# Bias rows in four row groups, the zero key's term inside pv, fewer waits, spare products, and a new order of all engines

## The chip, the cores and the metric

The kernel runs on one core of one Trainium2 chip. The core has five engines that run side by side and meet only through semaphores: TensorE (PE in the profile, with its weight loads as PEld), VectorE (DVE), ScalarE (ACT), GpSimd (POOL) and SyncE (SP), which here issues all the transfers. The metric is the device time of one execution in microseconds; less is better.

## The reference

One layer of an audio tower on x of shape 8 x 256 x 128 in float32. Cut to what matters:

```python
zf, zi, zh = x @ Wf + bf, x @ Wi + bi, x @ Wh + bh
diff = softplus(-zf) - softplus(-zi)
log_f, log_i = -softplus(diff), -softplus(-diff)
log_val = concatenate([log(0.5), log_i + log_g(zh)]); a_star = concatenate([0, log_f])
h = exp(a_star + cumlogsumexp(log_val - a_star))        # 257 rows: row 0 is new

n = layernorm(h)                                        # attention, 8 heads of 16
q, k, v = n @ q_w.T, ...kv of the other half of the batch...
h = h + softmax(q k / sqrt(128)) v                      # 257 keys, key 0 among them

n = layernorm(h)                                        # 16 experts, top 2, and a shared one
z = swiglu(n @ shared_w1 + b1) @ shared_w2 + b2
cw = two largest of softmax(n @ gate_w + gate_b), made to sum to 1
y = sum over experts of cw * (swiglu(n @ expert_w1 + b1) @ expert_w2 + b2)
h = h + y + z
```

As row 0 of h is the same 0.5 everywhere, its normalised row is zero: key 0 has score 0 and value 0, and adds only exp(-max) to each denominator. That is the zero key. The output's row 0 needs a small computation of its own for 8 columns (the pieces whose names begin with z and that carry no unit).

## The kernel before

Features lie on the 128 partitions, tokens along the free axis. The batch is cut into 4 units of two sequences (512 columns). A unit goes through three phases: the recurrence (`z`, `lsum`, `e3`, `lp`, `t`, `d`, `hg`, `l`, `al`, `w`, `mscan`, `dw`, `ed`, `sscan`, `lf`, `ef`, `h1`), the attention (`center`, `var`, `rs`, `xn`, `q`, `k`, `v`; then for each sequence s and half c of the keys or queries `mx` with row maxima `mr`, `mz`, the transpose `nmt`, `nm`, `e0`, scores `st`, exponentials `pt`, `o0`, `pv`, `den`, `on`, `h2`), and the experts (`center`, `var`, `gate`, `r1`, `rexp`, `r2`, `cwb`, then 13 chunks of gate and up halves `g` and `u` with their copies `ge`, `ue`, clips, `th`, `gg`, `vc`, `te`, seven `down` steps, `yo`, `out`, `store`). Unit 0 comes first, and later units are laid over it.

Each of these is a piece. The order in which an engine runs its pieces is written out in the table `AT`, one place per piece and engine, as a planner left it; `order()` sorts the pieces by it. `BANK_OF` gives each PSUM bank use its bank, in the order of PE. There are 8 banks; `ps.take` waits until the last user has released one. So no engine chooses anything at run time: each runs its list, and where its next piece waits, everything behind it waits as well.

A float32 product is issued as two passes on PE, each a weight load and a MATMUL; a gate or up half is three float32r products (high and low parts). Score products (`mx`, `st`) use 32 of the 128 rows of the array, four of them side by side in four row groups; `pv` products use 32 columns each, four side by side in four column groups. Other products use the whole array.

The weights `w1` arrive raw. For each of seven parts of up to 512 columns, `wp` adds on PE the bias row (a 2-row product with `bsel`) to the raw part (an identity product), and ACT and DVE split the sum into `w1h` and `w1l`. `o0` writes the zero key's part of the denominators, with all 128 columns of the array, into the bank in which `pv` then accumulates; it is a piece of its own with its own place in the order.

SP's queue issues, in this order: x of unit 0, the first constants, the other constants, x of unit 1, `w1a`, `w1b`, x of unit 2, `w2`, x of unit 3. Lines in the trace: L1146 is every ordinary product (`mm`), L1149 every transpose (`turn`), so tiles tell the pieces apart: `bank<-pt,cst` with 128*128 is the identity product of `wp`, `bank<-tr,cst` with 2*128 its bias product, `bank<-h,cst` the first `center`, `bank<-kt,qt` is `mx` and `bank<-qt,kt` is `st` (the stationary operand comes second), `bank<-e,cst` is `o0`, `bank<-pt,vpad` and `bank<-pt,cst` with 128*32 are `pv`, `xh` and `xl` with `w1h` and `w1l` the gate and up halves, `tr,w` the `down` steps, `zxs` is `zg` and `zy,w` is `zd`.

Of the kernel before, what the change touches and what calls it, by code (L numbers as in the profile page):

```python
# [51 lines left out]


# [5 lines left out]
def unit_pieces(u):  # L59
# [4 lines left out]
    for s in range(2):  # L64
# [14 lines left out]
    f += [("yo", u), ("out", u), ("store", u)]  # L79
    z = []  # L80
# [7 lines left out]
SETUP_PIECES = [(n, 0, k) for k in range(W1_PARTS) for n in ("wp", "w1h", "w1l")] + [("w2s", 0)]  # L88
# [14 lines left out]
def takes_part(engine, piece):  # L103
# [12 lines left out]
    if name in PART_BY:  # L116
# [21 lines left out]
    ),  # L138
# [58 lines left out]
def filled_by(piece):  # L197
# [1253 lines left out]
```

## Time and profile before

| | us |
|---|---|
| median of 3 runs | 304.44 |
| lowest and highest run | 303.33, 305.41 |
| the profiled execution, its own time | 303.86 |
| its span in the profile | 302.0 |
| PE busy | 275.3 |
| DVE busy | 239.7 |
| ACT busy | 188.6 |
| POOL busy | 118.4 |
| mean granted clock of PE, 1 is 2.4 GHz | 0.945 |

The profile is of one execution. Times in it count from the start of the span. The profiled execution took 1.86 us more than its span. A busy time says that an engine had work, not that the work was at full speed: the granted clock stands beside it.

### The profile page before, as it was taken

What the parts mean: (1) busy time and instruction counts of PE and PEld (TensorE: products, weight loads), DVE (VectorE), ACT (ScalarE), POOL (GpSimd) and SP (SyncE); (2) the same over time, 40 slices, a digit from 0 to 9 for tenths busy, and PEclk for the clock granted to TensorE, in tenths of its full rate; (3) what the DMA queues carried; (4) which work ended last, traced back from release to release, by engine and by line L of the source; (5) the groups of instructions that cost most, each with busy time, mean ns of one, the idle gap of its engine ahead of it and who ended that gap; (6) DMA issues with size and microseconds to landing.
All of it is one profiled execution on the core that took longest, in us unless ns stands there. A gap on an engine that the chain in (4) does not pass through costs nothing.

```text
span 302.0 us, 5217 instructions
## 1 busy us (share of the span) xinstructions
PE 275.3 (91%) x1766; PEld 167.0 (55%) x1766; DVE 239.7 (79%) x421; ACT 188.6 (62%) x298; POOL 118.4 (39%) x84
## 2 busy tenths in 40 slices
PE   2994996689989999989999999999979999999993
PEld 1421343446546775554676685447748659767641
DVE  1096645997499989889999699999887977689991
ACT  2849698969768766643688954636877485325051
POOL 2002546480041586063009176200943920391920
PEclk9995798579999999999999999999999996899998
DMA  6800000000000000000010000000000100000011
GB/s 226 358 0 0 0 1 1 2 0 2 2 0 4 0 2 0 0 3 0 2 36 3 0 2 2 0 0 3 0 2 1 37 0 2 1 0 0 2 35 35
DMA packets 3373, 5.78 MB, mean 19 GB/s; under 512 B 266, under 2 KB 2450, under 8 KB 3218
## 3 DMA queue, kind: packets, MB, share of 16 engines
q1 hardware_dynamic: 3348, 5.46, 5.0%
q8 instruction: 15, 0.25, 0.3%
q14 instruction: 10, 0.08, 0.1%
HBM read 4.40 MB, written 1.05 MB: 18 GB/s over the span
## 4 chain that ended last, share of the span: by engine, by line
PE 75%; DVE 11%; issue 7%; ACT 5%; DMA 1%; POOL 0%; DVEq 0%; SPq 0%; ACTq 0%; POOLq 0%
PE bank L1146 73%; DVE mxt L901 3%; PE bank L1149 2%; DVE tr L998 1%; DMA cst<-in_consts 1%; DVE yr L966 1%; ACT qt L635 1%; DVE tr L1018 1%; DVE qt L912 1%; DVE vr L976 1%; ACT pt L672 1%; DVE yo L1028 0%; ACT z L575 0%; ACT al L601 0%; DVE mxt L907 0%
## 5 line engine op out<-in xcount | busy, mean ns | idle before, releaser
L523 POOL TENSOR_TENSOR vr<-vr,cwb 128x1024 f32<-128x1024 f32 x24 | 63.3, 2652 | 16.5 <-DVE vr L976 14.0
L1146 PE MATMUL bank<-tr,w 128*128 128x512 f32 (+1 forms) x104 | 47.8, 599 | 0.0
L901 DVE TENSOR_REDUCE mxt<-bank 128x2 f32<-128x512 f32 x64 | 40.4, 685 | 9.3 <-PE bank L1146 9.0
L724 ACT ACTIVATE tr<-yr,fpar 128x1024 f32<-128x1024 f32 (+1 forms) x28 | 30.1, 1088 | 26.1 <-PE bank L1146 14.1
L1146 PE MATMUL bank<-xh,w1h 128*128 128x512 f32 x104 | 46.3, 446 | 0.0
L966 DVE TENSOR_SCALAR yr<-bank,fpar 128x512 f32<-128x512 f32 x52 | 39.4, 801 | 5.8 <-PE bank L1146 5.7
L1146 PE MATMUL bank<-xh,w1l 128*128 128x512 f32 x104 | 41.5, 400 | 0.0
L1146 PE MATMUL bank<-xl,w1h 128*128 128x512 f32 x104 | 41.5, 399 | 0.0
L998 DVE SCALAR_TENSOR_TENSOR tr<-tr,yr 128x1024 f32<-128x1024 f32 (+1 forms) x28 | 36.6, 1324 | 5.3 <-ACT tr L724 5.3
L672 ACT ACTIVATE pt<-bank 128x512 f32<-128x512 f32 x64 | 33.8, 602 | 9.1 <-PE bank L1146 9.1
L517 POOL TENSOR_SCALAR vr<-vr,fpar 128x1024 f32<-128x1024 f32 x12 | 15.2, 1267 | 48.6 <-ACT vr L711 48.6
L1018 DVE TENSOR_TENSOR tr<-tr,vr 128x1024 f32<-128x1024 f32 x24 | 31.8, 1338 | 0.3
L1146 PEld LDWEIGHTS bank<-tr,w 128*128 128x128 f32 (+1 forms) x104 | 19.1, 190 | 21.4 <-issue 20.0
L1146 PE MATMUL bank<-kt,qt 32*128 32x256 f32 x256 | 21.2, 449 | 7.7 <-DVE mxt L901 6.0
L1146 PEld LDWEIGHTS bank<-xh,w1h 128*128 128x128 f32 x104 | 20.0, 192 | 7.9 <-issue 4.4
L976 DVE TENSOR_SCALAR vr<-bank,fpar 128x512 f32<-128x512 f32 x28 | 21.6, 804 | 3.2 <-PE bank L1146 3.1
L1146 PE MATMUL bank<-pt,cst 128*32 128x256 f32 (+2 forms) x270 | 23.8, 390 | 0.0
L560 ACT ACT_TABLE_LOAD x18 | 23.1, 1283 | 1.0 <-PEq L1444 0.7
L1146 PEld LDWEIGHTS bank<-kt,qt 32*128 32x128 f32 x256 | 13.6, 209 | 17.7 <-issue 10.9
L1146 PEld LDWEIGHTS bank<-xl,w1h 128*128 128x128 f32 x104 | 20.0, 193 | 4.6 <-issue 1.2
L1146 PEld LDWEIGHTS bank<-xh,w1l 128*128 128x128 f32 x104 | 19.9, 191 | 4.7
L1146 PE MATMUL bank<-qt,kt 32*128 32x256 f32 x256 | 19.1, 414 | 3.4 <-DVE yr L966 1.9
(182 smaller groups left out, 431.9 us busy)
## 6 DMA issues: line engine op xcount, KB each, us to landing
pt<-in_w1a SPq DMA_DIRECT2D x1, 1672.0 KB, 9.2
xt<-in_x SPq DMA_DIRECT2D x4, 256.0 KB, 7.4
out<-osb SPq DMA_DIRECT2D x8, 128.0 KB, 1.9
w<-in_w SPq DMA_DIRECT2D x1, 832.0 KB, 10.7
cst<-in_consts SPq DMA_DIRECT2D x1, 552.5 KB, 5.1
cst<-in_consts SPq DMA_DIRECT2D x1, 193.5 KB, 4.2
tr<-in_w1b SPq DMA_DIRECT2D x1, 26.1 KB
out<-zo SPq DMA_DIRECT2D x1, 4.0 KB
```

Of the source, the lines that this page charges most:

```text
L517: g.tensor_scalar(v_, v_, fpar[:, UHI, r:r + 1], fpar[:, ULO, r:r + 1], ALU.min, ALU.max).then_inc(S["ucg"], 1)
L523: g.tensor_tensor(vr[:, n % NV, :, :], vr[:, n % NV, :, :], cwb[:, u % 2, :].unsqueeze(1).to_broadcast([P, 2, W]), ALU.mult).then_inc(S["v ...
L560: nc.scalar.add_instruction(mybir.InstLoadActFuncSet(name=nc.get_next_instruction_name(), act_func_set_id=number, ins=[], outs=[]))
L672: last = a(pt[:, n % NPT, 2 * t:2 * t + 2, :].rearrange("p i t -> p (i t)"), ps.bank("st", u, s, c, t)[:, :], ACT.Exp, scale=SCORE_SCALE)
L724: a(halves(k, tr, n % NT), halves(k, yr, n % NY), ACT.Tanh, scale=fpar[:, HA, r:r + 1]).then_inc(S["th"], 1)
L901: last = v.tensor_reduce(top_of, ps.bank("mx", u, s, c, t)[:, :].rearrange("p (i t) -> p i t", i=2), AX_X, ALU.max)
L966: last = v.tensor_scalar(yr[:, n % NY, c % 2, :], ps.bank("g", u, c)[:, :], fpar[:, GHI, r:r + 1], fpar[:, GLO, r:r + 1], ALU.min, ALU.max)
L976: last = v.tensor_scalar(vr[:, n % NV, c % 2, :], ps.bank("u", u, c)[:, :], fpar[:, UHI, r:r + 1], fpar[:, ULO, r:r + 1], ALU.min, ALU.max)
L998: v.scalar_tensor_tensor(t, t, 1.0, halves(k, yr, n % NY), ALU.add, ALU.mult).then_inc(S["gg"], 1)
L1018: v.tensor_tensor(t, t, halves(k, vr, n % NV), ALU.mult).then_inc(S["tev"], 1)
L1146: return nc.tensor.matmul(out_, lhsT, rhs, start=start, stop=stop, **k)
L1149: return nc.tensor.matmul(out_, data, ident, start=True, stop=True, is_transpose=True)
```

## The change

Five things.

1. `wp` becomes two pieces in place of seven: the identity products of four (then three) parts, then their bias products, part k in row group k mod 4. The bias rows `w1b` are laid out on partitions 0, 32, 64 and 96 and come by four transfers. `bsel` has its two rows in each row group.
2. `o0` is no longer a piece: `pv` with c = 0 takes the bank and writes the zero key's part by four products of 32 columns each.
3. A gate or up half waits for `xl` only if it is the first of its unit on PE, and for parts of `w1` only in unit 0.
4. Eight spare pieces in unit 0, each two products over 256 columns with the weights and x that lie there, into a bank that PE itself releases. Nothing reads the result. Each waits for one event, by `SPARE`.
5. The tables `AT` and `BANK_OF` are new throughout.

```diff
+SPARE = (("m", 2), ("s", 2), ("sq1", 1), ("rs1", 1), ("mz", 1), ("mz", 2), ("nm", 2), ("lden", 1))
...
-            a += [("o0", u, s)] * (c == 0) + [("pv", u, s, c)]
+            a += [("pv", u, s, c)]
...
+    if u == 0:
+        a += [("spare", 0, i) for i in range(len(SPARE))]
...
-SETUP_PIECES = [(n, 0, k) for k in range(W1_PARTS) for n in ("wp", "w1h", "w1l")] + [("w2s", 0)]
+SETUP_PIECES = [("wp", 0, 0), ("wp", 0, 1)] + [(n, 0, k) for k in range(W1_PARTS) for n in ("w1h", "w1l")] + [("w2s", 0)]
...
+FIRST_HALF = [next(p for p in order("P") if p[0] in "gu" and p[1] == u) for u in range(UNITS)]
...
-            sp.dma_start(w1_row, w1b_in).then_inc(s_w1b, 16)
+            for t in range(PAIRS):
+                sp.dma_start(w1_row[32 * t:32 * t + 2, :], w1b_in[2 * t:2 * t + 2, :]).then_inc(s_w1b, 16)
...
-            def wp(u, k):
+            def wp(u, g):
                 pe.wait_ge(s_const, 16)
                 pe.wait_ge(s_w1a, 16)
-                pe.wait_ge(s_w1b, 16)
-                ps.take(pe, "wp", 0, k)
...
-                mm(o, ident, w1_raw[:, cols], stop=False)
-                ps.fill(mm(o, const("bsel")[0:2, :], w1_row[:, cols], start=False), "wp", 0, k)
+                pe.wait_ge(s_w1b, 16 * PAIRS)
+                parts = range(PAIRS * g, min(PAIRS * g + PAIRS, W1_PARTS))
+                cols = [slice(k * W, min((k + 1) * W, W1COLS + E)) for k in range(W1_PARTS)]
+                for k in parts:
+                    ps.take(pe, "wp", 0, k)
+                    mm(ps.bank("wp", 0, k)[:, 0:cols[k].stop - cols[k].start], ident, w1_raw[:, cols[k]], stop=False)
+                for k in parts:
+                    n = cols[k].stop - cols[k].start
+                    rows = slice(32 * (k % PAIRS), 32 * (k % PAIRS) + 2)
+                    ps.fill(mm(ps.bank("wp", 0, k)[:, 0:n], const("bsel")[rows, :], w1_row[rows, g * W:g * W + n], start=False), "wp", 0, k)
+
+            def spare(u, i):
+                ge(pe, *SPARE[i])
+                ps.take(pe, "spare", 0, i)
+                o = ps.bank("spare", 0, i)
+                ps.fill(mm(o[:, 0:T], wtok[:, 0:P], xt[:, 0, 0:T]), "spare", 0, i)
+                ps.release(mm(o[:, T:W], wtok[:, 0:P], xt[:, 0, T:W]), "spare", 0, i)
...
-            def o0(u, s):
-                ps.released(pe, "nmt", u, s)
-                ps.take(pe, "o0", u, s)
-                ps.fill(mm(ps.bank("o0", u, s)[:, T:W], const("e0sel"), e0[:, s, :], start=True, stop=False, skip_group_check=True),
-                        "o0", u, s)
...
+                if c == 0:
+                    ps.released(pe, "nmt", u, s)
+                    ps.take(pe, "o0", u, s)
+                    for t in range(PAIRS):
+                        last = mm(o[32 * t:32 * t + 32, T:W], const("e0sel")[:, 32 * t:32 * t + 32], e0[:, s, :], start=True, stop=False,
+                                  skip_group_check=True)
+                    ps.fill(last, "o0", u, s)
...
-                ge(pe, "xl", u + 1)
-                for k in sorted({(2 * c + kind) * P // W, ((2 * c + kind + 1) * P - 1) // W}):
-                    ps.released(pe, "wp", 0, k)
+                if not AT or (name, u, c) == FIRST_HALF[u]:
+                    ge(pe, "xl", u + 1)
+                if u == 0:
+                    for k in sorted({(2 * c + kind) * P // W, ((2 * c + kind + 1) * P - 1) // W}):
+                        ps.released(pe, "wp", 0, k)
```

The tables, read out as orders, for the stretches of which the text speaks (a name, then the unit, then sequence and half or chunk):

```
PE before, from the start: z0.1 z0.0 z0.2 z1.0 lsum1 z1.2 lsum0 z1.1 wp0.2 wp0.1 wp0.0 wp0.3 center0.1 z2.1 z2.0
  var0.1 lsum3 z2.2 wp0.4 k0 wp0.6 z3.0 z3.1 wp0.5 lsum2 v0 q0 z3.2 mx0.0.0 mx0.0.1 mx0.1.0 mx0.1.1 nmt0.0
  center1.1 st0.0.0 var1.1 o00.0 nmt0.1 st0.0.1 pv0.0.0 st0.1.0 pv0.0.1 st0.1.1 k1 v1 q1 o00.1 pv0.1.0 mx1.0.0
  pv0.1.1 mx1.0.1 mx1.1.0 center0.2 center2.1 nmt1.0 var0.2 mx1.1.1 var2.1 o01.0 st1.0.0 gate0 nmt1.1 v2 g0.5
PE after: z0.0 z0.1 z0.2 z1.1 z1.2 lsum0 z1.0 lsum1 wp0.0 center0.1 spare0.1 spare0.0 spare0.2 var0.1 wp0.1 k0
  q0 spare0.3 v0 mx0.0.0 z2.0 z2.1 z2.2 lsum2 mx0.0.1 mx0.1.0 nmt0.0 spare0.4 st0.0.0 z3.1 st0.0.1 lsum3 z3.2
  mx0.1.1 z3.0 pv0.0.0 pv0.0.1 nmt0.1 spare0.6 spare0.5 center1.1 st0.1.0 spare0.7 var1.1 st0.1.1 pv0.1.0 k1 q1
  pv0.1.1 mx1.0.0 v1 mx1.0.1 center0.2 mx1.1.0 var0.2 nmt1.0 st1.0.0 mx1.1.1 gate0 st1.0.1 pv1.0.0 u0.0 u0.1 g0.0
  cwb0 g0.1
DVE after, from the start: t0 d0 l0 hg0 w0 mscan0 dw0 lf0 sscan0 h10 w2s0 w1l0.0 ... xn0.1 xsum0 w1l0.4 l1 w1l0.5
  w1l0.6 w1 mscan1 dw1 (mr0.0.0) sscan1 (mr0.0.1) mr0.1.0.0 mz0.0 mr0.1.0.1 nm0.0 mr0.1.0.2 mr0.1.0.3 l2
  mr0.1.1.0 w2 mr0.1.1.1 mscan2 dw2 mr0.1.1.2 mr0.1.1.3 mz0.1 sscan2 nm0.1
PE before, the end: ... down3.3 down3.4 down3.5 down3.6 out3, with zg after var3.2 and zd0 after u3.8
PE after, the end: down3.2 down3.3 zcw0 zg0.0 ... zg0.12 down3.4 down3.5 down3.6 out3 zd0 zout0
DVE after, the end: gg3.6 te3.6 zclip0 yo3 zgg0 zte0 zy0
```

In the order before, DVE runs `w2s0` ahead of `h10`, and ACT runs `ed0` ahead of `ef0`; after, both pairs are exchanged.

## Rows read from the trace of the kernel before

**Rows 1.** the page, part 1: busy us, share of the span, instructions

```profile
PE 275.3 (91%) x1766; PEld 167.0 (55%) x1766; DVE 239.7 (79%) x421; ACT 188.6 (62%) x298; POOL 118.4 (39%) x84
```

**Rows 2.** the page, part 4: the chain that ended last, by engine

```profile
PE 75%; DVE 11%; issue 7%; ACT 5%; DMA 1%; POOL 0%; DVEq 0%; SPq 0%; ACTq 0%; POOLq 0%
```

**Rows 3.** stages: us, busy us of PE, PEld, DVE, ACT, POOL; PE clock, DMA, GB/s

```profile
23.00:34.00 11.00, 6.78 (x9) 2.90 (x10) 7.29 (x12) 8.48 (x14) 5.52 (x4) 0.53 0.00 0
34.00:50.00 16.00, 14.31 (x52) 6.09 (x50) 7.18 (x13) 14.95 (x25) 7.75 (x6) 1.00 0.00 1
50.00:64.00 14.00, 10.28 (x68) 6.05 (x68) 13.34 (x24) 9.81 (x15) 8.32 (x6) 0.51 0.01 1
64.00:100.00 36.00, 33.29 (x344) 20.04 (x341) 28.63 (x65) 28.97 (x57) 8.73 (x9) 1.00 0.01 2
...
250.00:262.00 12.00, 12.00 (x58) 10.66 (x58) 7.71 (x36) 4.46 (x8) 1.70 (x2) 0.72 0.01 2
```

**Rows 4.** timeline of PE, 19 to 43 us: start, us, instruction, count, wait before

```profile
19.51 1.12 PE L1146 MATMUL bank<-tr,cst 2*128 2x512 f32 x2
...
21.62 1.12 PE L1146 MATMUL bank<-tr,cst 2*128 2x512 f32 x2
27.22 2.04 PE L1146 MATMUL bank<-h,cst 128*128 128x512 f32 x2 [4.48 <-issue]
...
41.42 1.02 PE L1146 MATMUL bank<-pt,cst 128*128 128x512 f32 x2
42.38 1.12 PE L1146 MATMUL bank<-tr,cst 2*128 2x512 f32 x2
```

**Rows 5.** timeline of DVE, 25 to 27 us

```profile
25.33 0.99 DVE L1035 TENSOR_SCALAR w<-w,fpar 128x1536 f32<-128x1536 f32 x1
...
26.44 0.68 DVE L864 TENSOR_TENSOR h<-state,rl 128x512 f32<-128x512 f32 x1
```

**Rows 6.** timeline of PE, the first score products

```profile
48.56 1.15 PE L1146 MATMUL bank<-kt,qt 32*128 32x256 f32 x16 [1.40 <-ACT vpad L655]
51.13 2.09 PE L1146 MATMUL bank<-kt,qt 32*128 32x256 f32 x16 [1.42 <-DVE mxt L901]
```

**Rows 7.** timeline of PE, 76 to 80 us

```profile
76.33 0.59 PE L1146 MATMUL bank<-e,cst 128*128 128x256 f32 x2
76.86 1.07 PE L1146 MATMUL bank<-pt,vpad 128*32 128x256 f32 x16
...
78.72 1.15 PE L1146 MATMUL bank<-kt,qt 32*128 32x256 f32 x16
79.80 1.07 PE L1146 MATMUL bank<-pt,vpad 128*32 128x256 f32 x16
```

**Rows 8.** the page, part 5: the row maxima on DVE

```profile
L901 DVE TENSOR_REDUCE mxt<-bank 128x2 f32<-128x512 f32 x64 | 40.4, 685 | 9.3 <-PE bank L1146 9.0
```

**Rows 9.** timeline of PE, where experts' products start, and two in between

```profile
94.84 0.48 PE L1146 MATMUL bank<-xh,w1h 128*128 128x512 f32 x1
...
127.42 0.39 PE L1146 MATMUL bank<-xl,w1h 128*128 128x512 f32 x1
127.65 0.39 PE L1146 MATMUL bank<-xh,w1l 128*128 128x512 f32 x1
...
149.93 0.50 PE L1146 MATMUL bank<-xh,w1h 128*128 128x512 f32 x1
```

**Rows 10.** timelines of PE and DVE, short z steps and the end

```profile
274.45 2.96 PE L1146 MATMUL bank<-zy,w 128*128 128x8 f32 x26
...
290.42 6.17 PE L1146 MATMUL bank<-tr,w 128*128 128x512 f32 x14
297.44 0.66 PE L1149 MATMUL bank<-cst,yo 128*128 128x128 f32 x4 [0.85 <-DVE yo L1028]
...
257.16 0.26 DVE L1094 SCALAR_TENSOR_TENSOR zy<-zy 128x104 f32<-128x104 f32 x1
...
296.63 0.75 DVE L1028 SCALAR_TENSOR_TENSOR yo<-bank,cst,h2n 128x512 f32<-128x512 f32 x1 [1.81 <-PE bank L1146]
```

More of the change, by code:

```diff
@@ L124 @@
     "P": (
[13 rows of a table removed]
[12 rows of a table added]
     ),
     "A": (
[10 rows of a table removed]
[10 rows of a table added]
     ),
     "V": (
[13 rows of a table removed]
[13 rows of a table added]
     ),
     "G": (
[3 rows of a table removed]
[3 rows of a table added]
     ),
     "S": (
-        0, 1, 3, 4, 2,
+        0, 1, 2, 3, 4,
     ),
@@ L203, in filled_by @@
         return [("y0", u)]
+    if name == "pv":
+        return [("o0", u, numbers[0])] if numbers[1] == 0 else []
+    if name == "wp":
+        return [("wp", 0, k) for k in range(PAIRS * numbers[0], min(PAIRS * numbers[0] + PAIRS, W1_PARTS))]
     if name == "zg":
         return [("zg", 0)] if numbers[0] == 0 else []
-    one_bank = ("wp", "z", "lsum", "center", "var", "q", "k", "v", "nmt", "o0", "gate", "cwb", "g", "u", "out",
+    one_bank = ("spare", "z", "lsum", "center", "var", "q", "k", "v", "nmt", "gate", "cwb", "g", "u", "out",
                 "zv", "zc", "zvar", "zgate", "zcw", "zd", "zout")
@@ L318, in build @@
         w1_raw = pt[:, :, :, :].rearrange("p a b c -> p (a b c)")[:, 0:W1COLS + E]
-        w1_row = tr[0:2, :, :, :].rearrange("p a b c -> p (a b c)")[:, 0:W1COLS + E]
+        w1_row = tr[:, :, :, :].rearrange("p a b c -> p (a b c)")[:, 0:2 * W]
         memory = [ctx.enter_context(nc.psum_tensor(f"bank{i}", [P, 512], F32)) for i in range(BANKS)]
@@ L1151, in _ @@
             wtok = const("wtok")
-            def wp(u, k):
+            def wp(u, g):
                 pe.wait_ge(s_const, 16)
                 pe.wait_ge(s_w1a, 16)
-                pe.wait_ge(s_w1b, 16)
-                ps.take(pe, "wp", 0, k)
-                cols = slice(k * W, min((k + 1) * W, W1COLS + E))
-                o = ps.bank("wp", 0, k)[:, 0:cols.stop - cols.start]
-                mm(o, ident, w1_raw[:, cols], stop=False)
-                ps.fill(mm(o, const("bsel")[0:2, :], w1_row[:, cols], start=False), "wp", 0, k)
+                pe.wait_ge(s_w1b, 16 * PAIRS)
[14 more added lines that the diff above has]
+                ps.release(mm(o[:, T:W], wtok[:, 0:P], xt[:, 0, T:W]), "spare", 0, i)
             def z_(u, j):
@@ L1370, in _ @@
             run("P", {"z": z_, "lsum": lsum, "center": center, "var": var, "q": q_, "k": k_, "v": v_, "mx": mx, "nmt": nmt,
-                      "st": st, "o0": o0, "pv": pv, "gate": gate, "cwb": cwb_, "g": gate_half, "u": up_half, "down": down,
-                      "out": out_, "zv": zv, "zc": zc, "zvar": zvar, "zgate": zgate, "zcw": zcw, "zg": zg, "zd": zd, "zout": zout, "wp": wp})
+                      "st": st, "pv": pv, "gate": gate, "cwb": cwb_, "g": gate_half, "u": up_half, "down": down,
+                      "out": out_, "zv": zv, "zc": zc, "zvar": zvar, "zgate": zgate, "zcw": zcw, "zg": zg, "zd": zd, "zout": zout, "wp": wp, "spare": spare})
 def layout(inputs):
@@ L1406, in layout @@
     shift = np.stack([np.zeros_like(shift), shift], axis=1).reshape(-1)
-    w1b = np.stack([w1[0], np.concatenate([shift, np.zeros(E, np.float32)])])
+    w1b = np.zeros((PAIRS, 2, 2 * W), np.float32)
+    for k in range(W1_PARTS):
+        cols = slice(k * W, min((k + 1) * W, W1COLS + E))
+        at = slice(k // PAIRS * W, k // PAIRS * W + cols.stop - cols.start)
+        w1b[k % PAIRS, :, at] = np.stack([w1[0], np.concatenate([shift, np.zeros(E, np.float32)])])[:, cols]
     w2e, w2s = f("L0_ffn_expert_w2")[:, :, perm], f("L0_ffn_shared_w2")[:, perm]
@@ L1423, in layout @@
     bsel = np.zeros((P, P), np.float32)
-    bsel[0, 1:] = -1.0
-    bsel[1, 0] = 1.0
+    bsel[0::32, 1:] = -1.0
+    bsel[1::32, 0] = 1.0
     parts = {
@@ L1435, in layout @@
     consts = np.concatenate([parts[n] for n in CONSTS], axis=1)
-    arrays = {"x": x, "consts": consts, "w1a": w1a, "w1b": w1b, "w2": w2.reshape(P, -1)}
+    arrays = {"x": x, "consts": consts, "w1a": w1a, "w1b": w1b.reshape(2 * PAIRS, -1), "w2": w2.reshape(P, -1)}
     return {k: np.ascontiguousarray(a) for k, a in arrays.items()}
```

99 rows, old and new, of tables (AT, BANK_OF, BY) are left out of this document.

## The prediction, made before the change was run

> **What bounds the kernel now.** I began with the page: TensorE (PE) is busy 275.3 of 302.0 us, VectorE (DVE) 239.7, ScalarE (ACT) 188.6 [rows 1], and the chain that ended last lies on PE for 75% and on DVE for 11% [rows 2]. A busy PE need not be a fast one, so the stages came next, with the granted clock beside them [rows 3]. Outside four stretches PE is full at the upper level, 2.4 GHz. The four are: from 23 to 34 us PE works 6.78 us, nearly all at half clock (1.2 GHz); from 34 to 50 it idles 1.7 us; from 50 to 64 it works 10.28 us at half clock and idles 3.7; from 64 to 100 it idles 2.7. Late, from 250 to 262, the granted clock is 0.72, so 6.7 us were at half. Half clock costs half of the busy time: 3.4 + 5.1 us in front, about 3.3 late. Idle in front is 8.1 us. So 16.6 us are to be had before 100 us, and anything elsewhere must come off PE's own work.
>
> Then the order of time. PE runs out of work at 22.74, idles 4.5 us, and resumes at 27.22 with the product that reads h1 of unit 0 [rows 4]. The other hole is the unit's row maxima: the first two batches of score products start at 48.56 and 51.13, behind waits of 1.40 and 1.42 us [rows 6], and two more like them follow by 57.6, the later ones waiting for the DVE reductions that free banks. DVE takes 0.69 us for each of 64 such reductions [rows 8], about 0.62 from start to start, so a batch of four costs it 2.5 us while PE needs 1.08 [rows 7]. PE is starved there, not full, and slow besides.
>
> **The change part by part.**
>
> *Bias rows in four row groups.* A product of 512 columns is two passes of 0.43 us (fourteen of them take 6.17 [rows 10]), 0.86 in all. An identity product that a bias product follows takes 0.96, and from one bias product over an identity product to the next it is 2.11 [rows 4], so a change of shape costs 0.19, there and back 0.39, of which the product behind bears 0.1 (left out below on both sides). Four of the seven parts stand ahead of the hole, 8.4 us in all up to 22.74, and three behind it, two of 2.0 and a short one of 1.2: 5.2. After, four identity products and one group of bias products cost 3.4 + 1.05 = 4.5, and the last three 2.2 + 1.05 = 3.2. That the group lasts as long as one product I take from the score products, whose 16 passes over 256 columns in four row groups take 1.08 [rows 7]: four at a time. The first saving, 3.9 us, only widens the hole in front of 27.22: it is worth nothing. The second is worth **-2.0**. Bound if the groups do not overlap: 0. The rows now come by four transfers in place of one, and the x of units 2 and 3 and w2 are queued behind three more issues on SP. The first of them is read after 40 us in the new order: hidden by the work in front; the four themselves are waited for ahead of the first identity product, at 14.3 us; should they land later, the hole behind covers 3.9 us and more.
>
> *The way to h1 of unit 0.* The scaling of w2 (1.27 us of DVE, from 25.33) stands ahead of the h1 product at 26.44 [rows 5]; now it stands behind. But ACT's exponentials are exchanged (ef before ed), which puts the second scan some 0.6 us later. I take the hole to end at 27.0; bounds 26.1 and 27.6. -0.2.
>
> *Spare pairs.* Each is two products over 256 columns, four passes of 0.215: 0.86 us at full clock, 1.7 at half. Eight are **+6.9** where PE is the bound, nothing in a hole. By their semaphores and places: numbers 1, 0 and 2 stand between center and var of unit 0, where PE would otherwise wait for ACT's square and then run at half clock; number 3 ahead of v; 4 behind the first nmt, in a wait for nm; 6 and 5 in a wait for nm; 7 ahead of var of unit 1. I count them all in and put what they fill into the idle time.
>
> *The new order.* I walked it with durations of the rows. center at 27.0; spares and var to 33.3 (clock up at about 31); the remaining parts to 36.5; k, q; a wait of 0.8 for ACT's copies; first scores at 40.8, where before had 48.56. Then three z and lsum of unit 2 (0.86 each) go between the score batches, where before had waits. The second batch ends at 46.4, DVE then needs five reductions and mz, 46.5 + 5 x 0.62 + 0.3 = 49.9, and PE is through with the third at 47.5: a wait of 2.5 ahead of nmt of sequence 0. The fourth batch ends at 57.4; four reductions (2.5) with w of unit 2 (0.7, as the h1 product of its size [rows 5]), the maximum scan and dw among them (my estimate 1.3 each, twice as much data) and mz end at 63.5, PE has done z and both pv by 62.0: a wait of 1.6 with nmt. Another of 1.3 comes before st of unit 1: idle 6.2 in all, so I take the clock to stay up after 31. The first expert product comes at 90.5, where before had 94.84 [rows 9], with the same sum of work done (it has pv and st of unit 1, before has v, center and var of unit 2). Then PE waits 1.8 us at cwb for DVE's r2, which before does not; but walked on, the first expert product of unit 1 comes at 147.9 with both st batches of unit 2 behind it, against 149.93 without them [rows 9]: 4.4 ahead. The same from sums: idle and half clock 16.6 now, 6.2 + 1.8 + 2.0 after, bias rows -2.0, spares +6.9, is 6.6 less gained and 4.9 more spent: -1.7. The walk says -4.4 and the sums -1.7, as the sums carry ends that are modelled. I take **-3.9**, nearer the walk, since it follows each wait; bounds -6.5 (the clock up from 28 on, no wait at cwb) and +1 (the stretch is slow as before and the spares are paid).
>
> *Zero key's part of the denominators.* Now two full products of 0.215 us ahead of pv, in a place of their own: 0.53 from start to start when pv follows [rows 7]. After, eight column-tile passes, four at a time: 0.43, no change of shape. Eight times -0.1 at most, where the old place had no shape change, 0: **-0.4**.
>
> *Fewer waits.* Each half of an expert product waited for xl and one or two weight parts. In the trace expert passes start 0.23 us apart [rows 9]; the waits are issued while the array works. **-0.2**, bounds 0 and -1. Behind the waiting half stands all of PE, but nothing that was waited for is late. Two more table loads come onto ACT, which is 62% busy [rows 1]: nothing.
>
> *The end.* Two moves, against each other. The 26 zg pairs (5.7 us, narrow) leave the start of unit 3's experts, where half clock followed (6.7 us of it [rows 3]), and come ahead of the last three down steps. The clock can fall there just so: 0 net, bounds -3.3 and +2. And zd moves from 274.45, where it took 2.96 us of a full PE, to the very end. Now the end is yo at 296.63, out at 297.44, copy, store: 5.4 us [rows 10]. After: yo, then two or three short z steps on DVE at 0.2 to 0.26 [rows 10] and two copies, zd 2.9, zy, zout, ACT, store: 8.0. Less 3.1 us of zd and zout taken out ahead: -0.5 at full clock, +2.4 at half, since PE idles before it. **+0.8**.
>
> Sum: -3.9 - 0.4 - 0.2 + 0.8 = -3.7 (the bias rows, the way to h1 and the spares are in the walk). The profiled execution is 303.86 us, 1.86 above its span and 0.6 below the median: 303.86 - 3.7 = 300.2, **300.7** as a median.
>
> **A rule against it.** The rows say that half clock costs 8.5 us in front, 2.8% of the span [rows 3]. The Trainium skill ("TensorE: Matmul & The Clock Gate", Part 1) says that the ramp penalty is under 1% of a typical kernel's span and need not be fitted. By that the spare pairs could win back 3 us at most for 6.9 us of work. The trace disagrees as to the size; how much of it the spares win back, no row shows.
>
> **The rivals.** *The clock stays low and the spares are paid.* The waits of 2.5 and 1.6 us let it fall again, as it fell at 50 us after waits of 1.4 us. Then the 5.1 us of that stretch come back: 305.8. For it: the order still waits for the same reductions. Against: eight z products now lie between them. *All of it works.* The spares lie in holes and the clock is up early (1.4 us more in front), and zg's half clock does not return (-3.3): 296.0. *Slower: DVE stands in line behind a late score batch.* In the new order mr of (sequence 1, half 1) heads DVE's queue while its score batch stands behind three z and lsum products on PE: by the walk DVE idles from 53.4 to 57.4, and w, the scans of unit 2 and l of unit 3 wait behind it. DVE has only 62 us to spare in 302 [rows 1]. If none of the 4 us is made up, and the end is at half clock, the time is 300.7 + 4 + 1.6 + 2 = 308.3; it decides once over 3 of the 4 us reach the last te. *The bias products do not run side by side*, as their banks and rows are separate but their passes are issued pair by pair: +1.9 behind the hole, 302.6.
>
> **How the numbers follow.** Forecast 300.7: 0.48 (own range 298.5 to 302.5). All works, 296.0: 0.20. Spares paid, 305.8: 0.15. Slower, 308.3: 0.10. No overlap, 302.6: 0.07. To hold 8 in 10 the range goes from 294.5 to 306. About 1% either way (301.4 and 307.5) is what a measurement here can tell from no change. Under 301.4: most of the forecast's case and all of the second, 0.54. Over 307.5: 0.10. Between: 0.36.
>
> **What would show it.** Right: bias products start four at a time, some 0.01 us apart; clock at 1.0 from 31 to 34 on through 64 us; first scores near 41, first expert product near 90; DVE idle near 53 to 57; the last store behind zd. Wrong: a second stretch at half clock between 45 and 65 us; var of unit 0 later than 34; PE idle above 8 us between 34 and 100; expert halves under 0.23 us a pass; a hole in the middle of unit 0's experts, where banks are held by gate halves that DVE reaches late.

## The result, and the profile after

The changed kernel took 309.34 us (median; 307.10 to 311.93), the kernel before 304.93 beside it: 1.0152 times as long, 95% interval 1.0077 to 1.0228. Forecast was 300.7. Medians are over all executions of a kernel, ratios over those within 1.5% of its fastest. The four executions lie in two pairs, 307.1 and 307.4 (mean granted clock 0.954), 311.2 and 311.9 (0.945 and 0.940); the profiled one (311.24, span 309.4) is of the upper pair, so some 4 us of what it shows are not in each of them.

The page: TensorE, VectorE and ScalarE do more than in [rows 1], and the chain that ended last now lies on VectorE for 23%, not 11% [rows 2].

```profile
PE 281.0 (91%) x1846; PEld 171.6 (55%) x1846; DVE 247.5 (80%) x421; ACT 191.8 (62%) x300; POOL 121.8 (39%) x84
...
PE 57%; DVE 23%; issue 13%; ACT 3%; DMA 1%; DVEq 1%; SPq 0%; ACTq 0%
```

VectorE is busy 7.8 us more with the same 421 instructions: the first sign that something holds it. The stages, to lay beside [rows 3]:

```profile
23.00:34.00 11.00, 6.35 (x15) 4.49 (x16) 6.45 (x11) 8.35 (x12) 4.48 (x3) 0.54 0.00 0
34.00:50.00 16.00, 14.28 (x83) 7.52 (x85) 12.53 (x21) 12.90 (x21) 4.04 (x4) 1.00 0.01 2
50.00:64.00 14.00, 10.67 (x74) 5.57 (x66) 7.69 (x11) 9.14 (x18) 7.25 (x5) 0.88 0.00 0
64.00:100.00 36.00, 31.40 (x324) 18.56 (x326) 27.91 (x53) 27.28 (x49) 15.15 (x12) 0.92 0.01 1
250.00:262.00 12.00, 11.94 (x49) 7.92 (x48) 11.51 (x31) 6.92 (x10) 3.46 (x3) 1.00 0.00 1
282.00:302.00 20.00, 19.42 (x72) 12.86 (x72) 14.84 (x23) 2.51 (x5) 5.62 (x2) 0.74 0.00 1
```

The clock is up from 34 us, where the walk had it at about 31. Then from 50 to 64 TensorE idles 3.3 us, and from 64 to 100 4.6 (2.7 before); half clock returns at 53 to 57, at 94 to 101, and near the end at 289 to 299, where before had 251 to 258. TensorE's timeline shows where the walk and the chip part:

```profile
18.67 1.13 PE L1157 MATMUL bank<-pt,cst 128*128 128x512 f32 x2 [1.52 <-DVE lt L833]
19.73 1.14 PE L1157 MATMUL bank<-tr,cst 2*128 2x512 f32 x8
27.65 2.04 PE L1157 MATMUL bank<-h,cst 128*128 128x512 f32 x2 [6.78 <-issue]
...
42.05 1.15 PE L1157 MATMUL bank<-kt,qt 32*128 32x256 f32 x16 [0.26 <-ACT qt L646]
...
49.44 1.15 PE L1157 MATMUL bank<-kt,qt 32*128 32x256 f32 x16 [1.44 <-DVE mxt L912]
53.58 0.69 PE L1160 MATMUL bank<-cst,mxt 128*128 128x128 f32 x2 [3.00 <-DVE mxt L918]
54.06 1.91 PE L1157 MATMUL bank<-xt,cst 128*128 128x256 f32 x4
```

The bias products do run four at a time: eight passes in 1.14 us. The first scores start at 42.05 (the walk: 40.8; before: 48.56 [rows 6]). Then nmt, the transpose of the maxima, of sequence 0 starts at 53.58, not 50.0, behind 3.00 us of idle time that ends with L918, the clamp of the maxima (mz). The spare pair behind it runs at half clock (1.91 us). VectorE and GpSimd at that place:

```profile
51.18 2.34 DVE L918 TENSOR_SCALAR mxt<-mxt 128x16 f32<-128x16 f32 x1
53.44 0.68 DVE L912 TENSOR_REDUCE mxt<-bank 128x2 f32<-128x512 f32 x1
...
63.07 0.69 DVE L912 TENSOR_REDUCE mxt<-bank 128x2 f32<-128x512 f32 x1 [6.03 <-PE bank L1157]
...
68.63 1.20 DVE L918 TENSOR_SCALAR mxt<-mxt 128x16 f32<-128x16 f32 x1
...
51.14 2.34 POOL L468 TENSOR_TENSOR z<-z,l 128x1024 f32<-128x1024 f32 x1 [4.16 <-ACT l L601]
53.45 1.26 POOL L469 TENSOR_TENSOR z<-z,l 128x512 f32<-128x512 f32 x1
...
68.52 1.27 POOL L492 TENSOR_TENSOR rl<-rl,al 128x512 f32<-128x512 f32 x1
```

A clamp of 128x16 elements takes 2.34 us, and it begins 0.04 us behind a GpSimd sum that takes 2.34, and ends 0.04 behind it. The group of its eight instances, shortest, median and longest in ns:

```profile
L918 DVE TENSOR_SCALAR mxt<-mxt x8: 171/182/2344, 51.2 to 210.3; 128x16 f32<-128x16 f32 x8
```

The second long one (1.20 us, at 68.63) runs beside a GpSimd subtraction and is in front of the other nmt, at 69.88 where the walk had 63.6. From there the lag stays: the first expert product starts at 102.7 (forecast 90.5, before 94.84 [rows 9]), that of unit 1 at 160.0 (147.9; 149.93). The Trainium skill ("SBUF — State Buffer", "SBUF: two separate sides") says that VectorE and GpSimd share one pair of SBUF ports as an exclusive lock: of a GpSimd instruction and a VectorE one that runs in a two-port mode or has two inputs in SBUF, the first to start has the pair for the whole instruction, and the other blocks. The trace agrees as to the blocking, by these two pairs of rows; in which mode the clamp, which has one input, runs, no row shows.

### The profile page after: what moved, and what is told of

It is laid out like the page before. It is cut to its first block, busy times and chain, and to the rows that moved or that the text cites. A ratio compares the mean times of both kernels' runs of the same rounds, so it can differ in the third digit from the quotient of the medians.

```text
span 309.4 us, 5305 instructions
## 1 busy us (share of the span) xinstructions
PE 281.0 (91%) x1846; PEld 171.6 (55%) x1846; DVE 247.5 (80%) x421; ACT 191.8 (62%) x300; POOL 121.8 (39%) x84
## 4 chain that ended last, share of the span: by engine, by line
PE 57%; DVE 23%; issue 13%; ACT 3%; DMA 1%; DVEq 1%; SPq 0%; ACTq 0%
PE bank L1157 56%; DVE yr L977 5%; DVE mxt L912 4%; DVE tr L1009 4%; DVE tr L1029 2%; DMA cst<-in_consts 1%; DVE vr L987 1%; DVE mxt L918 1%; PE bank L1160 1%; DVE qt L923 1%; DVE wm L847 1%; ACT tr L735 1%; ACT l L601 1%; DVE state L860 0%; DVE wm L840 0%
## 5 line engine op out<-in xcount | busy, mean ns | idle before, releaser
L1157 PE MATMUL bank<-tr,w 128*128 128x512 f32 (+1 forms) x104 | 51.5, 627 | 0.4 <-DVE tr L1029 0.3
L1009 DVE SCALAR_TENSOR_TENSOR tr<-tr,yr 128x1024 f32<-128x1024 f32 (+1 forms) x28 | 38.4, 1387 | 3.2 <-ACT tr L735 2.9
L1029 DVE TENSOR_TENSOR tr<-tr,vr 128x1024 f32<-128x1024 f32 x24 | 34.2, 1438 | 0.6
L528 POOL TENSOR_SCALAR vr<-vr,fpar 128x1024 f32<-128x1024 f32 x12 | 17.4, 1454 | 36.4 <-ACT vr L722 36.4
L1157 PE MATMUL bank<-xt,cst 128*128 128x256 f32 (+1 forms) x56 | 23.9, 569 | 5.7 <-DMA cst<-in_consts 5.7
L1157 PE MATMUL bank<-pt,cst 128*32 128x256 f32 (+1 forms) x270 | 22.9, 389 | 1.5 <-DVE lt L833 1.5
L722 ACT ACTIVATE vr<-bank 128x512 f32<-128x512 f32 x24 | 13.8, 601 | 14.0 <-PE bank L1157 13.7
L1157 PE MATMUL bank<-kt,qt 32*128 32x256 f32 x256 | 18.9, 409 | 3.2 <-DVE mxt L912 2.0
```

The source lines that it names most:

```text
L528: g.tensor_scalar(v_, v_, fpar[:, UHI, r:r + 1], fpar[:, ULO, r:r + 1], ALU.min, ALU.max).then_inc(S["ucg"], 1)
L722: last = a(vr[:, n % NV, c % 2, :], ps.bank("u", u, c)[:, :], ACT.Copy)
L1009: v.scalar_tensor_tensor(t, t, 1.0, halves(k, yr, n % NY), ALU.add, ALU.mult).then_inc(S["gg"], 1)
L1029: v.tensor_tensor(t, t, halves(k, vr, n % NV), ALU.mult).then_inc(S["tev"], 1)
L1157: return nc.tensor.matmul(out_, lhsT, rhs, start=start, stop=stop, **k)
```

## The experiments

Each was timed in three rounds beside the kernel before (303.7 to 304.4 in these groups); all are edits of the changed kernel unless said otherwise. Where an order is edited, its table of places is renumbered and each operation keeps its bank. Four readings of the loss stood against each other: VectorE's clamp waits for GpSimd; the spare pairs are paid; the end of the kernel costs it; the parts of the change gain nothing even by themselves.

**e1_no_spares.**

```
-        a += [("spare", 0, i) for i in range(len(SPARE))]
+        a += []
```

> The changed kernel without its eight spare pairs, all else in the same order and the same banks. 'Spares paid' (they are TensorE work in no hole, 0.86 us a pair at full clock, and the clock would stand as it does without them): 309.3 - 6.9 = 302.4, with the granted clock from 50 to 64 us still near 0.88. 'Spares earn their cost' (without them TensorE falls to half clock in the waits for the maxima): 308 to 311, with the granted clock from 50 to 64 us near 0.5 as in the kernel before, and again from 64 to 100. In between, 305 to 307: the three pairs ahead of var are paid and the later ones fill waits.

Measured: 309.11 (307.30 to 310.26), as with the pairs. From 50 to 64 us the granted clock is 0.76 (0.88 with them), and the later stations (first expert product, cwb) come 2.2 us earlier, not 6.9. All eight together earn what they cost, in this order. Both long clamps stand in it too (2.33 and 1.19 us).

**e2_pool_waits.**

```
 def t_(u):
     ge(pool, "l3", u + 1)
+    if u == 2:
+        ge(pool, "mz", 1)
 def lf(u):
     ...
     ge(pool, "lf", 2 * u + 1)
+    if u == 2:
+        ge(pool, "mz", 2)
```

> The changed kernel, but GpSimd starts its first sum of unit 2 (z + l) only after the clamp of the maxima of sequence 0, and the second subtraction into rl of unit 2 only after the clamp of sequence 1. In the changed kernel these clamps took 2.34 and 1.20 us where the six others take 0.18, each ending with the GpSimd operation beside it. 'DVE's clamp waits for GpSimd and TensorE waits for the clamp': the clamps take 0.2 us, the first nmt starts near 51.4 in place of 53.6 and the second some 3 us earlier than 69.9; TensorE idles 3 us less before 70 us, and the kernel takes 2 to 4 us less than the changed one. 'The clamp is long for another reason' (its input, or the modelled record): its length stays, no change. 'Given back': the clamps are short, but GpSimd's later start delays the scans of unit 2 and 3 and the time stays within 1 us.

Measured: 305.56 (302.00 to 307.56), 3.8 less than the changed kernel, and 1.0002 times the kernel before (0.9958 to 1.0046). The group of its eight clamps:

```profile
L922 DVE TENSOR_SCALAR mxt<-mxt x8: 171/182/184, 51.3 to 202.5; 128x16 f32<-128x16 f32 x8
```

TensorE's timeline around the first nmt:

```profile
49.55 1.15 PE L1161 MATMUL bank<-kt,qt 32*128 32x256 f32 x16 [1.45 <-DVE mxt L916]
51.52 0.44 PE L1164 MATMUL bank<-cst,mxt 128*128 128x128 f32 x2 [0.82 <-DVE mxt L922]
51.79 1.03 PE L1161 MATMUL bank<-xt,cst 128*128 128x256 f32 x4
```

And two stages:

```profile
50.00:64.00 14.00, 12.86 (x145) 6.84 (x142) 9.21 (x16) 12.68 (x24) 8.64 (x6) 1.00 0.01 1
64.00:100.00 36.00, 32.41 (x321) 19.93 (x314) 28.65 (x64) 29.14 (x52) 16.60 (x14) 1.00 0.01 2
```

No clamp is over 0.184 us, the 3.00 us of idle time are 0.82, the pair behind takes 1.03 at full clock, and half clock is gone from 34 to 282 us. In the profiled executions the first nmt comes 2.1 us earlier, the second 4.6, cwb of unit 0 7.7 (97.2 against 104.9): 3 us of waiting for GpSimd became 7.7 there, by half clock and the batch queued behind. These two executions are one of the changed kernel's upper pair and one of the fastest of this one; the fastest of each are 5.1 us apart, the medians 3.8. "The clamp is long for another reason" and "given back" are both refuted.

**e3_z_early.** The special rows' steps back where before had them (zcw behind cwb of unit 2, zg ahead of gate of unit 3, zd and zout between the first down steps).

> The changed kernel with the special rows' steps (zcw, zg, zclip, zth, zgg, zte, zd, zy, zout and their store) back where the kernel before has them: zcw behind cwb of unit 2, the thirteen zg ahead of gate of unit 3, zd behind the first down step of unit 3, zout ahead of the third. 'The tail costs it': half clock from 289 to 301 us and zd behind the last output are gone, 4 to 5 us, of which up to 3.3 return as half clock behind the zg products near 250 us: 305 to 308. 'The tail is only where earlier delays come out': within 1 us of the changed kernel.

Measured: 320.84 (318.18 to 323.80), outside both. zout, ahead of the third down step, made TensorE wait 4.36 us for its bank, which an up half held, and half clock came three times behind 250 us (257 to 267, 281 to 284, 299 to 305). TensorE's timeline:

```profile
300.35 0.59 PE L1157 MATMUL bank<-cst,zt 128*8 128x128 f32 x2 [4.36 <-DVE vr L987]
300.86 10.12 PE L1157 MATMUL bank<-tr,w 128*128 128x512 f32 x18
```

So it says nothing sure of the tail; it shows what a step can cost that is moved with its old bank.

**e4_parts_old_order.** The three parts of code in the order and banks of before, without pairs.

> The code of the changed kernel (bias rows in row groups, the zero key's part in column tiles inside pv, fewer waits) in the order and the banks of the kernel before, without spare pairs. 'The parts are worth what the prediction gave them and the order spoils it': -2.0 -0.4 -0.2 against the kernel before, 302.3, and the hole ahead of the h1 product grows from 4.5 to 8 us. 'The parts are worth nothing where they stand': 304 to 305, as what they save on TensorE only lengthens its waits for DVE before 64 us. 'Their code costs' (the four transfers, the wider first wait): above 306.

Measured: 308.12 (305.08 to 311.75), 1.0070 times before (1.0017 to 1.0123): nothing of the 2.6 us, but a loss. So they were taken apart, each alone in the kernel before.

**e5_row_groups_alone.**

```
-    mm(o, ident, w1_raw[:, cols], stop=False)
-    ps.fill(mm(o, const("bsel")[0:2, :], w1_row[:, cols], start=False), "wp", 0, k)
+    for k in parts: mm(..., ident, w1_raw[:, cols[k]], stop=False)
+    for k in parts: ps.fill(mm(..., const("bsel")[rows, :], ...), "wp", 0, k)
```

> The kernel before with the bias rows in row groups alone (the group of four at the place of the first weight part, the group of three at that of the fifth). The prediction: -2.0 against the kernel before, 301.7, all of it behind the hole. 'Nothing comes through' (the first scores stay at 48.6 us because the ScalarE and VectorE work of unit 0 and 1 sets them): within 0.5 us. 'The group of four is late and lets the clock fall' (it needs four banks at once, one of which VectorE frees late, so TensorE waits 2 us near 17 us and half clock begins at 19 as in the run of all three parts): 305 to 308.

Measured: 308.64 (305.18 to 310.98), 1.0109 times before (1.0033 to 1.0185). The timeline, TensorE's rows and one of ScalarE's:

```profile
19.84 1.13 PE L1148 MATMUL bank<-pt,cst 128*128 128x512 f32 x2 [1.88 <-DVE lt L824]
20.90 1.73 PE L1148 MATMUL bank<-tr,cst 2*128 2x512 f32 x8
...
37.84 1.13 PE L1148 MATMUL bank<-tr,cst 2*128 2x512 f32 x6
...
49.07 1.24 PE L1148 MATMUL bank<-kt,qt 32*128 32x256 f32 x8 [2.62 <-DVE lt L824]
...
39.00 0.60 ACT L568 ACTIVATE w1h<-bank 128x512 fp32r<-128x512 f32 x1 [1.47 <-PE bank L1148]
```

In a group every part is finished only when the last one is. ScalarE, which copies the parts, waits 1.47 us for the first of them, its later work moves back with it, and the first scores start at 49.07, behind a wait of 2.62 us, not at 48.56 [rows 6]: TensorE's 2 us turned into a longer wait. The group of four needs four banks at once besides, and waits 1.88 us for one.

That explains why nothing is gained, but not the loss. The profiled execution is the longest of the four (310.98), and at its first expert product it is 0.8 us behind the kernel before, as at cwb of unit 2. The rest comes later, with half clock where before has none (0.66 from 222 to 227 us, 0.57 from 280 to 288) and more of it from 252 to 266 (0.63, before 0.77). Why the clock falls there in this kernel stays open.

**e6_column_tiles_alone.**

```
-            a += [("o0", u, s)] * (c == 0) + [("pv", u, s, c)]
+            a += [("pv", u, s, c)]          # eight column-tile passes at its start
```

> The kernel before with the zero key's part in four column tiles at the start of pv alone. The prediction: -0.4, 303.3. 'It comes late' (the two products stood in gaps ahead of pv, now they are on its path, and the bank is taken later): +0.5 to +1. 'It alters where the clock falls': runs at 303 and, in part, at 306 or more.

Measured: 306.43 (303.96 to 309.40), 1.0035 (0.9996 to 1.0074). TensorE's timeline around 221 us, of the kernel before:

```profile
218.75 0.60 PE L1146 MATMUL bank<-e,cst 128*128 128x256 f32 x2
221.24 1.15 PE L1146 MATMUL bank<-qt,kt 32*128 32x256 f32 x16 [1.89 <-DVE yr L966]
```

The same place in this kernel:

```profile
221.74 2.09 PE L1147 MATMUL bank<-qt,kt 32*128 32x256 f32 x16 [2.31 <-DVE yr L967]
223.76 1.08 PE L1147 MATMUL bank<-e,cst 128*32 128x256 f32 x8
```

The two products had stood in a gap. Without them the gap is 2.31 us, not 1.89, the scores behind it run at half clock (2.09 for 1.15), and the next zg comes 2.1 us late. That the missing products let the clock fall is not shown: in e5 they are in place, the gap is 1.89 us as before, and half clock begins at the same scores (1.50 us at 222.05). Nor does one trace show in which executions it falls; they lie at 304.0 to 304.8, 306.4 to 306.7 and 309.3 to 309.4.

**e7_fewer_waits_alone.**

```
-                ge(pe, "xl", u + 1)
+                if not AT or (name, u, c) == FIRST_HALF[u]:
+                    ge(pe, "xl", u + 1)
```

> The kernel before without the repeated waits of the expert halves alone. The prediction: -0.2, bounds 0 and -1: 303.0 to 303.7. Rival 'no cost was there': the same as before and the same spacing of 0.23 us between expert passes.

Measured: 304.67 (302.81 to 305.63), 1.0005 (0.9974 to 1.0037). No cost was there.

**e8_batch_earlier.** With the waits of e2, mx of (sequence 1, half 1) moved ahead of z and lsum of unit 3.

> The changed kernel with GpSimd's two operations behind the clamps, and the fourth score batch (sequence 1, half 1 of unit 0) ahead of the z and lsum products of unit 3 instead of behind them. 'VectorE stands in line behind the late batch and that costs': the batch starts near 54 in place of 58.3, VectorE idles 4 us less from 50 to 64, nmt of sequence 1 starts 3 us earlier than 65.3, and the time falls by 1.5 to 3 us against the kernel without this edit (302.0 at best, 305.6 median). 'VectorE's idle time there costs nothing, TensorE is full anyway': within 0.7 us of it, the other products merely change places.

Measured: 313.08 (312.96 to 315.96). The batch waited 3.4 us for a bank that lt of unit 2 held, and st behind it 3.8 for the banks of the batch. The edit made two waits of its own, so whether VectorE's line behind the late batch costs anything stays open. No theory foresaw it.

**e9_zg_between.** With the waits of e2, the zg steps between the down steps of unit 2, their VectorE and ScalarE steps with them.

> The changed kernel with GpSimd's two operations behind the clamps, and the thirteen zg steps one to three at a time between the first five down steps of unit 2 (with zcw, zclip, zth, zgg and zte moved ahead with them; zd, zy and zout stay last). 'Half clock follows a block of narrow products': with the block gone no stretch at half clock follows between 240 and 300 us and the last 3.3 us come back: 298.7 at best. 'Half clock comes for another reason, the waits of TensorE near the end or the time since the last stretch': a stretch of about 7 us at half clock stands there still; 302 or more. 'The narrow products spread are as bad': half clock near 242 to 250.

Measured: 308.18 (306.68 to 309.50). There was no half clock from 32 to 286 us, but at 287 it came. TensorE's timeline:

```profile
281.34 3.84 PE L1161 MATMUL bank<-tr,w 128*128 128x512 f32 x8 [0.30 <-DVE tr L1033]
291.13 5.39 PE L1161 MATMUL bank<-tr,w 128*128 128x512 f32 x8 [5.96 <-DVE tr L1033]
```

zg had filled a wait of TensorE for VectorE's last products. Taken away, the wait is bare (5.96 us), and zg's 5.7 us are paid ahead of it. The change had put zg where it costs least.

**e10_waits_no_spares, e12_last_five, e13_first_three, e15_last_five_no_waits.** Subsets of the eight pairs; the first three with the waits of e2, the last without.

```
-        a += [("spare", 0, i) for i in range(len(SPARE))]
+        a += [("spare", 0, i) for i in (3, 4, 5, 6, 7)]    # e12, e15; (0, 1, 2) in e13, none in e10
```

> The changed kernel with GpSimd's two operations behind the clamps of the maxima, and without the eight spare pairs. With both in place 302.0 at best and 305.6 as a median. 'The spares only fill waits, and with shorter waits they cost': 2 to 4 us less than with them, 299 to 302. 'The spares hold the clock': the granted clock from 50 to 64 us falls to 0.8 or less again and the time is 303 to 307.

> The changed kernel with GpSimd's two operations behind the clamps, without the first three spare pairs (the ones between center and var of unit 0). With all eight 305.6 (302.0 at best), with none 306.5 (306.2 at best). 'The later five hold the clock through the waits of 50 to 75 us, the first three are paid': 0.5 to 2 us less than with all eight, 303.6 to 305. 'The first three bring the clock up earlier': 1 to 2 us more, 306.5 to 307.5.

> The same, but with the first three spare pairs alone. 'The later five hold the clock': without them it falls at 52 and at 70 us as with none, 306 or more. 'The later five are paid': 304 or less, and no second stretch at half clock before 80 us.

> The changed kernel without its first three spare pairs and nothing else: GpSimd's two operations are free to start beside the clamps again. The fourth corner of a square: all eight and the clash 309.3, all eight and no clash 305.6, last five and no clash 302.2. 'The two add up' (3.7 for the clash, 3.3 for the first three pairs): 306. 'The clash decides where the clock falls, whatever the first three do': 308 to 309, with a clamp of 2.3 us and half clock near 52 and 92. 'Without the first three the clash does not happen' (VectorE and GpSimd meet elsewhere): 302 to 303 and clamps of 0.2 us.

Measured, medians in us:

```
pairs kept      with the waits of e2       without them
all eight       305.56 (302.00 to 307.56)  309.34 (307.10 to 311.93)
none            306.51 (306.16 to 309.01)  309.11 (307.30 to 310.26)
first three     307.48 (307.22 to 309.99)
last five       302.24 (301.19 to 304.56)  306.57 (305.80 to 311.13)
```

The last five take 4.3 us off against none, the first three add 1.0; against all eight, dropping the first three takes off 3.3 with the waits and 2.8 without, and the waits are worth 3.8 and 4.3 (2.6 with no pairs). The ratios to the kernel before (1.0002, 1.0062, 1.0114, 0.9935 down the first column; 1.0152, 1.0156, 1.0070 down the second) make it 4.6, 4.1 and 2.9 us for the waits, 2.0 and 2.5 for the first three, 3.9 for the last five with the waits and 2.6 without: the same signs, sizes to 1 or 2 us. So waits and the first three add up, and the last five seem worth more where the clamps are short. Why, in two stages of the kernel with none (e10):

```profile
50.00:64.00 14.00, 12.52 (x118) 6.30 (x122) 7.98 (x14) 11.43 (x23) 8.31 (x6) 0.88 0.01 1
64.00:100.00 36.00, 29.68 (x296) 16.39 (x289) 26.52 (x61) 27.10 (x50) 14.31 (x12) 0.91 0.01 1
```

And of the one with the last five (e12):

```profile
50.00:64.00 14.00, 12.72 (x134) 6.66 (x134) 9.26 (x18) 12.69 (x24) 9.47 (x6) 1.00 0.00 1
64.00:100.00 36.00, 33.11 (x314) 20.89 (x315) 27.90 (x62) 29.03 (x52) 16.79 (x13) 1.00 0.01 1
```

Pairs that stand in the waits for the maxima keep the clock up there. Those between center and var do not: TensorE is at half clock already (1.7 us a pair), and in e12 var starts at 30.7 in place of 34.0, the first scores at 40.9 in place of 42.2, cwb at 95.9 in place of 97.2 (e2). In the profiled executions these 1.3 us are lost again at the end, where e12 is at half clock from 280 to 291 us and e2 from 282 to 290; both spans are 300.4. The medians differ by more because every execution of e12 stays at or under 304.6 us. **e12_last_five is 0.9935 times the kernel before (0.9897 to 0.9973): faster than both kernels**, by little.

**e11_narrow_weighing.** With the waits of e2; nearly all of the weighing by the router is left out.

```
-  g.tensor_tensor(vr[:, n % NV, :, :], vr[:, n % NV, :, :], cwb[...] over W columns, ALU.mult)
+  g.tensor_tensor(vr[:, n % NV, :, 0:8], vr[:, n % NV, :, 0:8], cwb[...] over 8 columns, ALU.mult)
```

> The changed kernel with GpSimd's two operations behind the clamps, and GpSimd's weighing of the up halves (24 operations on 1,024 columns, 2.3 us each and up to 2.8 beside VectorE's) on 8 columns a half only: it leaves out nearly all of the weighing by the router, and all else stays. 'VectorE pays for the port all through the experts, and the end pays with it': VectorE's gate and up products (1.51 and 1.44 us on average, 1.21 alone) take 1.21, it is busy 12 us less, and the kernel gains 3 us or more, most of it behind 250 us: 299 to 302. 'TensorE is full there, the port costs nothing but at the end': 1 to 2 us. 'No cost': within 1 us of the kernel without this edit (median 305.6, best 302.0).

Measured: 302.31 (301.16 to 307.02). VectorE's two groups of products in e2:

```profile
L1013 DVE SCALAR_TENSOR_TENSOR tr<-tr,yr 128x1024 f32<-128x1024 f32 x24 | 35.9, 1508 | 2.9 <-ACT tr L739 2.6
L1033 DVE TENSOR_TENSOR tr<-tr,vr 128x1024 f32<-128x1024 f32 x24 | 34.2, 1439 | 0.6
```

The same two in this kernel:

```profile
L1033 DVE TENSOR_TENSOR tr<-tr,vr 128x1024 f32<-128x1024 f32 x24 | 29.5, 1241 | 0.6
L1013 DVE SCALAR_TENSOR_TENSOR tr<-tr,yr 128x1024 f32<-128x1024 f32 x24 | 29.1, 1218 | 3.4 <-ACT tr L739 3.1
```

VectorE loses 11.5 us to GpSimd's weighing in the experts. Yet the best executions differ by 0.8 us (301.2 and 302.0), the two profiled ones by 0.1 in span, and the fourth down step of unit 3 starts 1.4 us earlier: TensorE is full there, so little of it comes through. The median differs by 3.3, as fewer executions had a low mean clock (three of ten under 0.96, six of ten in e2). That sets 0.1 to 3.3, no closer.

**e14_pairs_in_zg.** With the waits of e2, two more pairs behind the fourth and the ninth zg.

> The changed kernel with GpSimd's two operations behind the clamps, and two more spare pairs among the thirteen zg steps (behind the fourth and the ninth), 1.7 us of full-width work in the block after which the clock fell at 282.9. 'Half clock follows a block of narrow products': it stays at full speed from 279 to 296 us, the 3.3 us come back against 1.7 spent, about 1.5 less: 300.5 at best. 'It falls for another reason': the stretch of half clock is still there and the kernel takes 1.7 us more, 303.7 at best.

Measured: 307.51 (306.21 to 310.89), 2 us more than without them. Half clock begins at 281, 3 us behind the start of the block (2.6 to 4.6 in the other traces with one unbroken block, e6 apart), one pair notwithstanding, and lasts to 294. So two full-width pairs do not prevent it. With e9, where no run of narrow products is longer than twelve and the clock falls in the wait: it comes with a block of narrow products and with an idle wait alike, and what would hold it up at the end isn't settled.

## Why the prediction was wrong

**The step that failed** is a term of the walk: "DVE then needs five reductions and mz, 46.5 + 5 x 0.62 + 0.3 = 49.9", and the like for sequence 1. The clamp took 2.34 and 1.20 us, since the new order lets GpSimd's sum and subtraction of unit 2 start just ahead of it; in before that sum began 0.2 us after the clamp had begun. 3.2 us more in front of two products for which TensorE waits gave 7.7 at cwb of unit 0 in the profiles, and 3.8 (e2 against the change; 4.3 by e15 and e12) in the median. That is shown by e2 and e15, and it is the whole loss against the kernel before, by the ratio of e2 (1.0002, 0.9958 to 1.0046); its median is still 1.9 us above it. The view to look at was there, of the same eight clamps before:

```profile
L907 DVE TENSOR_SCALAR mxt<-mxt x8: 151/174/917, 58.0 to 203.4; 128x16 f32<-128x16 f32 x8
...
160.07 0.92 DVE L907 TENSOR_SCALAR mxt<-mxt 128x16 f32<-128x16 f32 x1
...
158.52 2.43 POOL L517 TENSOR_SCALAR vr<-vr,fpar 128x1024 f32<-128x1024 f32 x2 [11.31 <-ACT vr L711]
```

A time of 0.9 for 0.17 of work needs a reason, and it stands beside it: that clamp, too, ends 0.04 us behind a GpSimd operation. I had walked TensorE, VectorE and ScalarE, not GpSimd.

**The walk without the clash.** Short clamps do not bring the forecast -3.9 for the stretch. In e2, with all eight pairs as in the walk:

```profile
94.96 0.50 PE L1161 MATMUL bank<-xh,w1h 128*128 128x512 f32 x1
...
152.23 0.50 PE L1161 MATMUL bank<-xh,w1h 128*128 128x512 f32 x1
```

The walk had these two at 90.5 and 147.9, the kernel before at 94.84 and 149.93 [rows 9]. By the walk's own measure, which gives 2.4 us for the score batches ahead of the second, e2 gains 0.1 us on before and not 4.4, and e12 (150.98) 1.3. Of the 4.5 us that the first is late, 1.4 stand at the first scores (42.16 for 40.8), as the clock rose at 34 us and not at 31; 0.3 come up to the second nmt (65.29); 2.7 lie between it and the expert product, at full clock, where TensorE idles 2.85 us and the walk had one wait of 1.3. The other 1.1 of that is work, and where the walk lost it stays open. So the clamps are the loss against before, but only one part of the miss of 8.6 us against the forecast.

**The clock.** "So I take the clock to stay up after 31": it rose at 34, fell at 53 and at 94, and with the clamps short it stays up from 34 to 282. The rival "the clock stays low and the spares are paid" (305.8, 0.15) is half right: it fell, but behind the clamps.

**Spare pairs**, "+6.9, all counted": wrong as one number. The first three cost 2 to 3 us, by median or ratio. The last five give 4 by the clock that they hold. The Trainium skill ("TensorE: Matmul & The Clock Gate", Part 1) has the ramp penalty under 1% of a typical kernel's span. None against last five, 306.51 to 302.24, is 1.4%: for this kernel, in which the clock falls more than once, the measurement decides against it.

**Bias rows**, "-2.0" behind the hole: wrong: alone they cost 3.3 us by the ratio of e5 (1.0 to 5.6), in whose one trace the parts' later end shows as 0.5 to 0.8 and half clock late in the kernel as the rest. I took a TensorE that is busy for the bound. Its own row said otherwise: the first scores stood behind ScalarE's vpad [rows 6], and ScalarE waits for the parts. Side by side they run, as said; the rival against that is refuted.

**Zero key's part**, "-0.4": +1.1 by the ratio of e6, an interval that just includes 0. The bound "where the old place had no shape change, 0" was no bound: it left out that the products filled a gap; whether that is what it costs is not shown.

**Fewer waits**, -0.2: none (e7), within its bounds.

**The hole** ends at 27.65, not 27.0, at the bound of 27.6.

**The end**, +0.8 with bounds -3.3 and +2 about zg: half clock moved from 251 to 258 us, where 3.3 us were lost, to 289 to 299, where 5.0 were. +1.7 for it, inside the bounds. zd came last at full clock, 3.1 us.

**The slower rival** gave 308.3, close to the time. Its sign was there, VectorE idle 6.03 us before the late batch (forecast 4.0); but e2 leaves the batch at its place in the order, VectorE still idles 4.7 us around there, and the loss is gone, so it isn't the cause of the loss; what it adds is open after e8.

**The best of it**, e12, is 2 us under the kernel before. It has three pairs fewer than the forecast, which reckoned them at 2.6 us, and is still 1.5 over 300.7.

## What to carry to other kernels

A walk needs every engine whose instructions can touch the path, GpSimd among them: for each short VectorE step from SBUF on the path, ask what GpSimd starts just then. Two waits of some 0.5 us on GpSimd took off 3.8. In a group of equal instructions look at the longest, not only at the mean. A saving on a busy engine counts only if its consumers don't wait for something else; what grouping saves, it may take back by finishing every part last. In this kernel work without use paid in the waits in which TensorE would have dropped its clock, and only cost where the clock was already down.

## What the hardware showed that I had not expected

- VectorE waits out the whole GpSimd instruction: a clamp of 0.17 to 0.18 us takes 2.34, ending 0.04 us behind the GpSimd operation. VectorE's reductions from PSUM beside GpSimd keep their 0.68. Products of SBUF tensors in e2 take 1.22 in the median, but 1.51 and 1.44 on average and up to 2.8 and 3.2.
- Executions of one kernel fall into groups some 2 to 3 us apart, each with its mean granted clock: e2 has four at 302.0 to 303.0 (mean clock 0.961 to 0.965), four at 305.4 to 305.8 (0.950), two at 307.4 to 307.6 (0.945). A group more or less is worth as much as most edits here, and an order can be judged only by many executions.
- TensorE, busy without a gap, dropped to half clock in a block of narrow products (zg, 16 and 8 columns) in every trace that has them in one block, 2.6 to 4.6 us behind its start; only in e6 the block was through first, and the clock fell 5.5 us behind its start.
